# The last chunk's front part by pairs of tiles, with some scores made before the last pair's keys

## The reference

```python
x = x + attn_a(layernorm(x))   # a state-space recurrence, see below
x = x + ffn(layernorm(x))      # one 128x128 product (ternary weights) and a bias
x = x + attn_b(layernorm(x))   # attention over the 8 rows, at each position apart
x = x + ffn(layernorm(x))
```

## Time and profile before

| | us |
|---|---|
| median of the runs shown | 612.39 (611.85 to 613.84) |
| the profiled execution's own time | 614.66 |
| its span | 612.9 |
| PE, DVE, ACT, POOL busy | 528.9, 470.5, 482.2, 415.5 |

### The profile page before, as it was taken

One profiled execution on the slowest core, in us unless ns is written; L12 is line 12 of the kernel. 1 busy time (PEld: TensorE's weight loads), 2 busy tenths in 40 slices (PEclk: granted clock), 3 DMA queues, 4 the chain that ended last, 5 costly groups with the idle time before them and its releaser, 6 DMA issues.

```text
span 612.9 us, 13462 instructions
## 1 busy us (share of the span) xinstructions
PE 528.9 (86%) x3960; PEld 441.5 (72%) x3960; DVE 470.5 (77%) x1085; ACT 482.2 (79%) x1478; POOL 415.5 (68%) x548
## 2 busy tenths in 40 slices
PE   4978999999999898897999898899988888878177
PEld 4857888888787777786887777688767666666166
DVE  6765666686669999976669999986669999732985
ACT  3799999999988888797988879699988898642001
POOL 7358778877768877785768877786776867422421
PEclk9989999999999998998999999999999999977688
DMA  8741221223201111212200111323111111100001
GB/s 203 210 124 39 73 96 57 75 82 101 67 25 38 59 57 58 94 60 73 75 30 36 59 58 59 90 62 93 59 57 59 53 50 52 35 18 1 0 1 35
DMA packets 52324, 39.43 MB, mean 64 GB/s; under 512 B 7317, under 2 KB 48026, under 8 KB 52250
## 3 DMA queue, kind: packets, MB, share of 16 engines
q1 hardware_dynamic: 44858, 34.86, 18.8%
q10 hardware_dynamic: 7392, 3.67, 2.1%
HBM read 33.44 MB, written 4.46 MB: 62 GB/s over the span
## 4 chain that ended last, share of the span: by engine, by line
PE 31%; DVE 29%; ACT 20%; issue 13%; POOL 3%; DMA 2%; DVEq 1%; ACTq 0%; POOLq 0%; SPq 0%
ACT turned L856 6%; ACT turned L871 6%; PE ps L1513 5%; DVE lmat L1182 4%; DVE area L1289 3%; PE ps L1682 3%; PE ps L1650 3%; ACT area L925 3%; PE ps L1840 3%; DVE state L1221 2%; PE ps L1736 2%; PE ps L1745 2%; DVE area L1276 2%; DVE mmat L1190 2%; DVE area L1272 2%
## 5 line engine op out<-in xcount | busy, mean ns | idle before, releaser
L871 ACT ACTIVATE turned<-ps,sct 128x128 f32<-128x128 f32 x376 | 110.6, 447 | 0.0
L856 ACT ACTIVATE turned<-ps,sct 128x128 f32<-128x128 f32 x368 | 103.1, 439 | 5.4 <-DMA sct<-packed 3.9
L1182 DVE TENSOR_TENSOR_SCAN lmat<-arow,band 128x512 f32<-128x512 f32 x64 | 84.2, 1320 | 6.1 <-POOL band L625 6.1
L604 POOL TENSOR_TENSOR cn<-turned 128x256 f32<-128x256 f32 x64 | 55.6, 869 | 47.0 <-ACT turned L871 47.0
L1190 DVE TENSOR_TENSOR mmat<-ps,lmat 128x512 f32<-128x512 f32 x64 | 43.9, 686 | 45.3 <-PE ps L1650 45.0
L762 ACT ACTIVATE area<-ps 128x256 f32<-128x256 f32 (+1 forms) x68 | 35.3, 580 | 55.1 <-PE ps L1840 26.6
L1650 PE MATMUL ps<-cT,bT 128*128 128x128 f32 x512 | 69.8, 280 | 8.6 <-DVE state L1221 5.9
L1650 PEld LDWEIGHTS ps<-cT,bT 128*128 128x128 f32 x512 | 63.7, 193 | 15.8 <-issue 14.6
L604 POOL TENSOR_TENSOR bn<-turned 128x256 f32<-128x256 f32 x64 | 52.3, 817 | 32.0 <-PE ps L1682 22.5
L1555 PE MATMUL ps<-w_sel_hi,xt_hi 128*128 128x512 f32 x128 | 59.7, 467 | 0.3 <-ACT turned L871 0.3
L1682 PE MATMUL ps<-wu,bn 128*128 128x128 f32 x384 | 54.5, 286 | 3.5 <-DVE mmat L1190 3.4
(11 more groups left out here) (238 smaller groups left out, 1420.3 us busy)
## 6 DMA issues: line engine op xcount, KB each, us to landing
arow<-alpha_rows SPq DMA_DIRECT2D x32, 512.0 KB, 3.6
drow<-decay_rows SPq DMA_DIRECT2D x64, 128.0 KB, 3.0
area<-in_L_attn_a_x_dram SPq DMA_DIRECT2D x4, 512.0 KB, 6.2
xT_rows<-turned SPq DMA_DIRECT2D x4, 512.0 KB, 5.3
xt<-xT_rows SPq DMA_DIRECT2D x32, 64.0 KB, 2.5
area<-in_L_attn_a_x_dram ACTq DMA_DIRECT2D x8, 256.0 KB, 2.9
out_dram<-area ACTq DMA_DIRECT2D x6, 256.0 KB, 2.4
area<-L_attn_a_sel_proj_w_dram SPq DMA_DIRECT2D x2, 512.0 KB, 6.4
```

Source lines behind the costliest of these rows:

```text
L604: pool.tensor_tensor(out[:, 0], zc[:, 0], zs[:, 1], ALU.subtract)
L856: last = act.activation(dst[h][:, N * q:N * q + N], bank(BK_B)[:, N * q:N * q + N], ACT.Copy, scale=scalars(c, k)[:, at + HH * h + q:at + ...
L871: last = act.activation(dst[h][:, N * q:N * q + N], bank(BK_C)[:, N * q:N * q + N], ACT.Copy, scale=scalars(c, k)[:, at + HH * h + q:at + ...
L1182: dve.tensor_tensor_scan(lmat[h], arow[i2][:, HH * P * h:HH * P * (h + 1)], band[h], 0.0, ALU.mult, ALU.add).then_inc(l_dve, 1)
```

## The change

**The front part of the last chunk** goes by four pairs p of two tiles, each with its own buffers, banks and semaphores (all names that begin with `h`), so that pair 0 can start at unit 10.75, when tile 1 is done. x for it comes in one load of 512 KB at the head of the last chunk's loads on SP, where two of 256 KB stood on ACT's queue (at 520.35 and 537.02 us). The old pieces (`x1:g` ... `Q1`) are not emitted for the last chunk any more. `f_alone` goes, and `WARM_LAST` is 1 in place of 2.

**Scores.** Queries 0 to 5 are multiplied by blocks: (first query, end, first key row, end). Three blocks are GpSimd's and two DVE's (`EARLY`), and two more, with the last pair's keys, DVE's (`LATE`). Queries 6 and 7 are GpSimd's whole. **Values:** GpSimd makes rows 2, 3, 4, 5, DVE 0, 1, 6, 7. **Order:** `attended(0)` and `attended(1)` stand behind the folds, `v 1` behind the second maximum, and ACT's second exponential ahead of its copies.

**All chunks:** the table's numbers and the spans differ a little, so that some pieces change places with the recurrence's steps: PE's two FFN products, on POOL one score product and `band`, on DVE the copy `oraw` and two products of attention, on ACT the copy `xt_hi`.

```diff
-WARM_STATS, WARM_NORM, WARM_SCALARS, WARM_ANGLE, WARM_LAST = 4, 1, 4, 2, 2
+WARM_STATS, WARM_NORM, WARM_SCALARS, WARM_ANGLE, WARM_LAST = 4, 1, 4, 2, 1
-PLACE = {"rr:0": 11.467, "load:0": 13.741, "x1:0": 14.931, "var0:0": 15.533, "xn0:0": 15.815, "T0": 15.9,
+PLACE = {"hrms:0": 10.75, "hx1:0": 10.786, "rr:0": 11.296, "hroot0:0": 11.407, "hnorm0:0": 11.441,
+ENDING = {name for name in PLACE if not name.startswith("h")}
+EARLY = [(0, 2, 0, 4), (2, 4, 0, 4), (0, 4, 4, 6), (4, 6, 0, 4), (4, 6, 4, 6)]
+EARLY_ON_GPSIMD = 3
+LATE = [(0, 4, 6, 8), (4, 6, 6, 8)]
-TG = numbered([("q", 3), ("q", 7), ("v", 2), ("v", 3), ("ve", 0), ("rs", 0), ("ve", 1), ("rs", 1), ("v", 4),
+TG = numbered([("q", 7), ("q", 6), ("v", 2), ("v", 3), ("v", 4), ("v", 5), ("ve", 0), ("rs", 0), ("ve", 1), ("rs", 1),
                ("ve", 2), ("rs", 2), ("ve", 3), ("rs", 3)])
+            sp.dma_start(x_end, x_rows[NC - 1]).then_inc(hx_in, 16)
             for b in range(NB):
                 tile_loads(NC - 1, b)
# GpSimd
+            def f_hrms(c, p):
+                pool.wait_ge(o_dve, NB * c + 2 * p + 2)
+                pool.tensor_tensor(rr_h[:, pair(p)], oraw[:, pair(p), D], eps_rms[:, pair(p)], ALU.add).then_inc(hg[p], 1)
...
+                pool.tensor_tensor(rr_h[:, pair(p)], rr_h[:, pair(p)], mhalf[:, pair(p)], ALU.pow).then_inc(hg[p], 1)
+            def f_hproduct(c, m):
+                q0, q1, r0, r1 = EARLY[m]
+                n, r = q1 - q0, r1 - r0
+                pool.wait_ge(hq_act, 1)
+                for p in range((r1 + 1) // 2):
+                    pool.wait_ge(ha[p], HEAD_A[p]["K"])
...
-            scores_of(3)
             scores_of(7)
-            pool.wait_ge(ta, TA["V"])
+            scores_of(6)
...
             values_of(2)
             values_of(3)
+            values_of(4)
+            values_of(5)
             root_of(0)
             root_of(1)
-            values_of(4)
# DVE
+            def f_hx1(c, p):
+                dve.wait_ge(hg[p], HEAD_G[p]["rr"])
+                dve.wait_ge(hx_in, 16)
+                for s in range(2 * p, 2 * p + 2):
+                    last = dve.scalar_tensor_tensor(x_end[:, s], oraw[:, s, 0:D], rr_h[:, s:s + 1], x_end[:, s], ALU.mult, ALU.add)
+                last.then_inc(hv[p], 1)
+                head_statistics(p, "x1", "st0")
+            def f_hproduct(c, m):
+                q0, q1, r0, r1 = EARLY[m]
+                for p in range((r1 + 1) // 2):
+                    dve.wait_ge(ha[p], HEAD_A[p]["K"])
+                for p in range((q1 + 1) // 2):
+                    dve.wait_ge(hp[p], HEAD_P["Q"])
...
+                some_scores(prod[:, m % 2], q0, q1, r0, r1).then_inc(h_sums[m], 1)
...
             scores_of(0)
+            sum_scores(0)
+            shift_of(0)
             scores_of(1)
-            sum_scores(0)
-            scores_of(2)
             sum_scores(1)
-            sum_scores(2)
-            sum_scores(3)
-            shift_of(0)
...
             weights(0)
...
             values_of(0)
+            sum_copied(7)
+            sum_copied(6)
+            shift_of(1)
             values_of(1)
-            scores_of(5)
...
-            attended(0)
-            attended(1)
             weights(1)
-            values_of(5)
             values_of(6)
             values_of(7)
             fold(6, 512, "v", "a")
             fold(7, 512, "v", "a")
             fold(6, 256, "a", "h")
             fold(7, 256, "a", "h")
+            attended(0)
+            attended(1)
# PE
-                if f_alone(("T", t), c):
-                    for name in ("stats", "var"):
-                        pe.wait_ge(f_v[g], v_step(name + norm[2], c))
-                        keep_warm(WARM_LAST, BK_T)
+            def f_hturn(c, k, p):
...
+                elif k == 0:
+                    pe.wait_ge(cT_act, UNITS * NC)
+                    for name in ("x1", "st0", "mv0"):
+                        pe.wait_ge(hv[p], HEAD_V[name])
+                        keep_warm(WARM_LAST, BK_T)
+                elif p == 3:
+                    pe.wait_ge(hv[p], HEAD_V["st1"])
+                    keep_warm(WARM_LAST, BK_T)
+                pe.wait_ge(hn[p], k + 1)
...
-            add_rows(2, 5, NB)
-            end_tick(add_rows(2, 4, NB), ("acc", 2))
+            add_rows(2, 4, NB)
+            end_tick(add_rows(2, 5, NB), ("acc", 2))
```

More of the change, by code:

```diff
@@ new lines, in f_hvals, with f_hrow, f_hnorm @@
+            def f_hvals(c, p):
+                act.wait_ge(hp[p], HEAD_P["KV"])
+                evac(vals_last[:, pair(p), :], kv_bank[p].rearrange("p (s e) -> p s e", s=2)[:, :, D:2 * D]).then_inc(ha[p], 1)
+            def f_hrow(c, p):
+                act.wait_ge(hp[p], HEAD_P["Q"])
+                evac(q_last[:].rearrange("p s e -> p (s e)"), bank(BK_T)[:, 2 * D:4 * D]).then_inc(ha[p], 1)
+            def f_hnorm(c, k, p):
+                act.wait_ge(hg[p], HEAD_G[p][f"sh{k}"])
+                if p >= 2 and k == 0:
+                    act.wait_ge(f_pe[1], use_done(("T", 7), c - 1))
+                for s in range(2):
+                    at = 2 * p + s
+                    last = act.activation(head_xn[p][:, s], x_end[:, at], ACT.Identity, bias=sh_h[:, at:at + 1], scale=rs_h[:, at:at + 1])
+                last.then_inc(hn[p], 1)
@@ L947, in f_load @@
+            place(pieces, "hrow:3", lambda c: in_ending(c) and f_hrow(c, 3))
             def f_load(c, g):
@@ new lines, in f_hreduce @@
+            def f_hreduce(c, m):
+                dve.wait_ge(h_sums[m], 1)
+                some_sums(g_ring[m] if m < EARLY_ON_GPSIMD else prod[:, m % 2], *EARLY[m]).then_inc(h_sums[m], 1)
+            pieces = []
+            for p in range(4):
+                place(pieces, f"hx1:{p}", lambda c, p=p: in_ending(c) and f_hx1(c, p))
+                place(pieces, f"hadd:{p}", lambda c, p=p: in_ending(c) and f_hadd(c, p))
+            for k in range(2):
+                place(pieces, f"hnorm{k}:3", lambda c, k=k: in_ending(c) and f_hnorm(c, k, 3))
@@ L1320, in _ @@
+            for m in range(len(EARLY)):
+                if m >= EARLY_ON_GPSIMD:
+                    place(pieces, f"hprod{m}", lambda c, m=m: in_ending(c) and f_hproduct(c, m))
+                place(pieces, f"hred{m}", lambda c, m=m: in_ending(c) and f_hreduce(c, m))
             for g in range(2):
@@ L1759, in _ @@
+            pieces = []
+            for p in range(4):
+                for k in range(2):
+                    place(pieces, f"hT{k}:{p}", lambda c, k=k, p=p: in_ending(c) and f_hturn(c, k, p))
+                place(pieces, f"hF:{p}", lambda c, p=p: in_ending(c) and f_hffn(c, p))
+                place(pieces, f"hKV:{p}", lambda c, p=p: in_ending(c) and f_hkv(c, p))
+                place(pieces, f"hQ:{p}", lambda c, p=p: in_ending(c) and f_hquery(c, p))
             for what, q in USES[0] + USES[1]:
```

340 lines of the change are left out of this document (219 added, 121 removed), and 53 rows, old and new, of tables (PLACE, TV).

## The result

The changed kernel takes 605.65 us (median of 4 runs, 604.26 to 608.52) against 613.12 us of before (4 runs, 611.85 to 613.96). The ratio is 0.988, 95% interval 0.9843 to 0.9916; a second set of six runs gave 605.74 us and 0.9882 (0.9846 to 0.9917). It is faster by 1.2%, 7.5 us in the medians: the sign is the forecast one (599.4 us, -13.0), the size little more than half of it, and the time lies just outside the range of 595 to 605.

A forecast was written before the change was run, and what follows sets the result against it. From the last tile on, the kernel was taken as a chain of single engines in four stretches: -1.1 - 8.5 - 7.9 + 4.5 = -13.0 us, from the median 612.39 to 599.4 us, range 595.0 to 605.0.

The forecast's parts named there:

- Stretch 1: Up to the last tile's `w_out` product, which waits for `ysum`: -1.1 us, bounds 0 and -1.3.
- the pieces that trade places: All chunks, pieces changing places with the recurrence's steps: put at nothing, may be -1 to +1 us for 64 units.
- case C: Pieces of pairs 0 to 2 in units 10 to 15 hold up the recurrence's queues: +2 to +5 us, 603; chance 0.12.
- Stretch 2: From the last `w_out` product to the first scores, bound by PE's work: -8.5 us, 24.95 less 16.4.
- Case A: Lower clock stays through the pair stage, with 16 unread transposes instead of 48: 6 us, 605.4; chance 0.13.
- Stretch 3: From the first scores to the folds' end, DVE's work falling from 34.9 to 27.1 us: -7.9, bounds -6.5 to -8.5.
- The cover named for it: Behind the folds, DVE waits 2 us for PE, which hides folds grown by about 1 us.
- Stretch 4: From the folds' end to the span's end, PE adding up rows late: +4.5 us, bounds +2.1 and +11.
- case B: Clock comes back earlier in stretch 2 or 4: up to -3.6 and -2.4 us, likelier half, 596.4; chance 0.15.
- Case E: Early scores bring nothing because the last pair's keys come late: 601 to 602 us; chance 0.04.
- Case D: Lower clock level through the whole ending: +17 us in all, 616.4; chance 0.06.

## Why the prediction was wrong

The sign and most of the mechanisms were right; the sum was off by 5.3 us in the profiles and 5.5 in the times, with two large terms in it. (The time itself is off by 6.3, since the kernel before was at 613.12 by four runs and not at 612.39.)

**Stretch 1, -1.1 forecast, +2.2 measured.** The term itself came true: the last tile's product waits for the sum of squares alone, -1.0. The step that failed is what was put at nothing in the recurrence: the pieces that trade places ("for 64 units that may be -1 to +1"), and with them pair 0's x1, which the sum left out and case C argued away. That argument looked at the free DVE of 520 to 540 us. But pair 0's x1 stands at 496, and there DVE has no gap up to the next scan. By the starts of the same scans, mean of two profiles each, the other 3.2 us come thus: 0.7 up to the scan near 486, which is less than the 3.0 between the two profiles of before; 1.0 from there to `xt_lo`, by the load and PE's level, which change with the execution; 1.3 from `xt_lo` to the next scan, pair 0's x1 (1.0, by the kernel that has it later) and the new order (0.3); 0.2 behind. So about 1.3 of it is shown as the change's own. The rest is mostly in the first profile: over the seven profiles of kernels that are the same up to the ending the last `w_out` product comes at 539.6 to 543.3, in the mean at 540.8, which is +1.5. The pieces' places alone cost 1.5 us by the timing (-0.2 to +3.2).

**Stretch 2, -8.5 forecast, -5.7 measured.** The mechanism was right: PE's own work bounds it, and DVE's first product waited for L1956. Two sizes were not. A pair's product was priced at half of a half's, "0.45, and a bias 0.2": it took 0.64 and 0.21. With six of them that is 1.2 us, and over the nine profiles with the 16 transposes this stretch is 18.3 us in the mean, not 16.4; the other 0.7 was not taken apart. And the subtrahend, 24.95 us, was one execution in which the last keys ran at the lower level; the second has 23.28, the kernel with only other places 21.68. The forecast took where the level stood in one profile for a property of the program.

**Case A** (the lower clock stays, fewer transposes) was priced at 6 us and given 0.13. By its own sign it did not occur: the granted clock of 545 to 556 us was 0.66 and 0.74 in the two profiles of after, not under 0.6, though it was 0.95 in before. But without any transposes some 3 us of it appear, and with twice as many perhaps 1.5 to 2.7 go. It is not a case beside the forecast but a part of it, in each execution to another degree, and the sum should have held some of it.

**Stretch 3, -7.9 forecast, -6.9 measured.** The terms were right but for one: the folds beside GpSimd took 1.2 us more, where "about 1 us" was expected and put at nothing. With it the folds end 28.3 us behind the first product, just over the 28 named as the sign that this sum is wrong. The cover named for it was to be a wait of 2 us on DVE. In the first profile 0.85 us of that is left, in the second none. Still the end does not move by it: in both PE works without a gap from row 1's passes to the third output product. The Trainium skill, "SBUF — State Buffer", section "Who interferes with whom", has the two exclude each other for the whole instruction, and here the trace agrees to 0.1 us: GpSimd's last product ended at 584.43 + 3.90 = 588.33, the four folds take 1.9 by themselves, and they ended at 590.14.

**Stretch 4, +4.5 forecast, +2.7 measured.** The chain is the one named (row 1's values, 48 passes, two output products, 32 passes, the third), and row 1's values ahead shorten it. From the first of the 48 passes to pair 2's first addition it is 15.6 us in the first profile, 15.3 forecast, and 13.7 in the second, where the 48 passes take 5.62 us and not 7.7: there the level came back sooner, which is case B for this stretch. The 32 passes took 3.84 us in both, 3.5 forecast at the full level. The mis-sized term is how much of the chain the folds cover: 7.5 us in both, not 6.5, since the folds themselves were longer. So the 1 us that stretch 3 lost is won back here. (The upper bound, +11, is +12.0 by its own terms.)

**Case C** did not occur as described: DVE's scans from 521.85 to 533.75 are as far apart as before to 0.2 us, so no pair's root held them up. Its price came in part by another way, as said under stretch 1. **Case E** did not occur: PE had the last pair's keys at 564.0, DVE needed them at 568.98. **Case D** did not either: the 32 passes and what follows ran at the full level.

## What to carry to other kernels

Before a sum is made against one profile, ask which of its rows stand at the lower clock and whether they must: two executions of one program differed by 1.7 us in one stretch and by 2.7 in the span. Price small matrix products by a row of their own size or by start to next start, with the bias that comes ahead, not as a share of a larger group. When work is moved in an ending, the engine that idled for it (here PE, 12.9 us) starts slow, and what is released late on the other engine, here one product of 1.2 us, sets the start of a long chain: move that first. And where an engine stands with no releaser named, set its start beside the landings of the loads that it reads: here that named the load of `sct` at once. A third buffer for it, so that it could be issued earlier, was not tried.

## What the runs showed of the hardware

A jump back to a loop's start held PE's queue for 3.8 us, in before and in after alike (3.4 to 4.0 over all fourteen profiles), where leaving the loop took 0.08. PE then went on 0.4 us after the branch in before and 3.1 to 3.8 us after it in all other kernels, also in the one that has the old places in the loop. What holds it there was not settled.

A load of the same kind at the same place took 1.8 to 3.6 us from issue to landing, 1.8 and 2.9 in two executions of one program, and ACT's instruction that reads it began within 0.1 us of the landing each time.

Additions of GpSimd beside two scans of DVE took 1.76 and 1.64 us in place of 0.73, and the scans 2.83 in place of 2.3. All four were done in 3.4 us, from 486.49 to 489.85, where one after the other they take 3.8: only some 0.4 us of it went on at the same time.

The granted clock went to different levels at the same instruction after the same idle time: the last `w_out` product took 2.07 us in one execution of the kernel before and 1.16 in another, both after 2.68 us of waiting.
